# Moving the source-block one-hot rows behind a group's additions in the two edge layers of a graph network

## The reference, cut to what matters

```
def _rgcn_layer(x, W, SW, b, src, dst, rel):
    xt = jnp.einsum('nd,rde->rne', x, W)
    msg = xt[rel, src]
    agg = jax.ops.segment_sum(msg, dst, num_segments=x.shape[0])
    return jax.nn.relu(agg + x @ SW + b)
...
x = _rgcn_layer(x, w1, sl1, b1, src, dst, rel)
x = _rgcn_layer(x, w2, sl2, b2, src, dst, rel)
```

## Time and profile before

| | us |
|---|---|
| median of 3 runs | 9071.17 |
| lowest and highest | 9058.99, 9072.06 |
| span of the profiled execution | 9059.0 |
| time of the run that fits that execution | 9058.99 |
| gathers of layer one start, first to last | 120.3 to 2250.7 |
| gathers of layer two start, first to last | 2276.0 to 4383.8 |

### The profile page before, as it was taken

How to read it: one execution, slowest core, us unless ns; L and a number is a source line. 1 busy time by engine, 2 the same in 40 slices (tenths; PEclk the granted TensorE clock), 3 DMA queues, 4 the chain that set the end, 5 groups by cost and what they waited for, 6 DMA issues and landing times. The chain is left out here.

```text
span 9059.0 us, 172600 instructions
## 1 busy us (share of the span) xinstructions
PE 6437.7 (71%) x29604; PEld 5123.3 (57%) x29605; DVE 5894.2 (65%) x18020; ACT 2567.4 (28%) x6875; POOL 6592.5 (73%) x6759
## 2 busy tenths in 40 slices
PE   6555555555688888888788888888745666666657
PEld 4443333333455555555588888887635555555555
DVE  4444444444566666666688888888845666666667
ACT  3111111111011111111355555555433333333322
POOL 6777777777777777777677777777667777777752
PEclk7556666666555555555555555555556777777778
DMA  5222222222222222222355555555435665666653
GB/s 196 60 64 64 64 64 64 65 64 62 52 61 62 62 62 62 62 62 62 96 136 137 136 136 136 136 137 136 121 78 129 152 150 144 155 150 149 149 135 78
DMA packets 1031683, 926.16 MB, mean 102 GB/s; under 512 B 210913, under 2 KB 911477, under 8 KB 1031495
## 3 DMA queue, kind: packets, MB, share of 16 engines
q0 software_dynamic: 214496, 443.25, 17.7%
q1 hardware_dynamic: 627671, 341.67, 14.8%
q10 hardware_dynamic: 189400, 139.98, 7.5%
HBM read 734.34 MB, written 192.49 MB: 102 GB/s over the span
## 5 line engine op out<-in xcount | busy, mean ns | idle before, releaser
L597 PE MATMUL stage_ps_agg<-stage_hot,stage_msg 128*128 128x128 f32 x6656 | 1562.7, 409 | 1349.4 <-DMA stage_msg<-xt,stage_index 1004.4
L597 PEld LDWEIGHTS stage_ps_agg<-stage_hot,stage_msg 128*128 128x128 f32 x6656 | 1355.4, 302 | 1632.4 <-issue 624.3
L1613 POOL DMA_INDIRECT slots<-big,stage_index x1664 | 1656.3, 995 | 512.5 <-issue 449.9
L586 POOL DMA_INDIRECT stage_msg<-xt,stage_index x1664 | 1624.6, 976 | 530.0 <-issue 472.3
L1157 POOL DMA_INDIRECT big<-q,stage_index x1664 | 1594.4, 958 | 546.9 <-issue 490.2
L586 POOL DMA_INDIRECT stage_msg<-xt_next,stage_index x1664 | 1601.9, 963 | 531.1 <-issue 513.7
L621 DVE TENSOR_TENSOR big<-big,stage_ps_agg 128x128 f32 x3328 | 952.6, 286 | 1432.0 <-PE stage_ps_agg L597 1072.2
L575 ACT ACTIVATE stage_index<-big 128x4 int32 (+1 forms) x832 | 170.2, 205 | 3698.9 <-PE stage_ps_agg L597 3655.7
L1656 PE MATMUL stage_ps_val<-nodes_a,big 128*128 x3328 | 665.6, 362 | 506.1 <-ACT big L1576 481.7
L1656 PEld LDWEIGHTS stage_ps_val<-nodes_a,big 128*128 128x128 f32 x3328 | 566.2, 257 | 549.8 <-issue 544.5
L1666 PE MATMUL stage_ps_sums<-stage_hot,big 128*128 128x128 f32 x4160 | 737.1, 343 | 107.5 <-DVE big L1784 101.4
(11 more groups left out here) (302 smaller groups left out, 9639.0 us busy)
## 6 DMA issues: line engine op xcount, KB each, us to landing
big<-slots SPq DMA_DIRECT2D x1976, 66.0 KB
big<-in_edge_attr_dram SPq DMA_DIRECT2D x1664, 64.0 KB
stage_trow<-targets ACTq DMA_DIRECT2D x830, 128.0 KB
stage_msg<-xt,stage_index POOLq DMA_INDIRECT x1664
stage_msg<-xt_next,stage_index POOLq DMA_INDIRECT x1664
big<-q,stage_index POOLq DMA_INDIRECT x1664
slots<-big,stage_index POOLq DMA_INDIRECT x1664
xt_next<-stage_xo SPq DMA_DIRECT2D x98, 256.0 KB, 2.9
```

The lines of the kernel that those rows point to most:

```text
L586: pool.indirect_dma_start(self.msg[q][:, j, :], None, self.xt, bass.IndirectOffsetOnAxis(ap=self.index[q][:, j:j + 1], axis=0))\
L597: last = self.nc.tensor.matmul(self.ps[h][:, j, :], self.msg[q][:, j, :], self.hot[h][:, j, :], start=True, stop=True)
L1613: pool.indirect_dma_start(d["slots"], bass.IndirectOffsetOnAxis(ap=index[q][:, j:j + 1], axis=0), total[q][:, j, :], None).then_inc(s_sc[q ...
```

## The change

In both layers DVE makes `hot` of group x + 1 first as before, then adds group x, and only then makes `block_hot` of group x + 1. The waits that stood ahead of `block_hot` go with it, and in layer two `base` goes with it too. The added test of `x.edge(1)` is decided while the program is built. No instruction is added or taken away.

```diff
@@ first layer, DVE
             if x.edge(1):
                 v.wait_ge(a.s_freed, x.at(1) + SLOTS - 1)
                 a.make_hot(v, x)
-                if x.edge(-1):
-                    v.wait_ge(s_met, x.at(-1) + 1)
-                a.make_block_hot(v, x)
             if x.edge():
                 if x.near == 0:
                     v.wait_ge(s_clear, 1)
                 a.add_sums(v, x)
+            if x.edge(1):
+                if x.edge(-1):
+                    v.wait_ge(s_met, x.at(-1) + 1)
+                a.make_block_hot(v, x)
             if x.job(SUM):
@@ second layer, DVE
                 h = x.slot(1, 2)
                 v.wait_ge(a.s_freed, x.at(1) + SLOTS - 1)
                 a.make_hot(v, x)
-                if x.edge(-1):
-                    v.wait_ge(s_rank, x.at(-1) + 1)
-                    v.wait_ge(s_pick, x.at(-1) + 1)
-                a.make_block_hot(v, x)
-                nc.vector.tensor_scalar(base[h][:, :], t["ident"][0:W, 0:W], begin[:, bass.ds(x.at(1), 1)], None,
-                                        ALU.mult).then_inc(s_base, 1)
             if x.edge():
                 a.add_sums(v, x)
                 h = x.slot(0, 2)
@@
                 nc.vector.tensor_reduce(t["slot_of"][:, bass.ds(x.at() * G, G)], pick[:, :, :], AX.X, ALU.add)\
                     .then_inc(s_kept, 1)
+            if x.edge(1):
+                h = x.slot(1, 2)
+                if x.edge(-1):
+                    v.wait_ge(s_rank, x.at(-1) + 1)
+                    v.wait_ge(s_pick, x.at(-1) + 1)
+                a.make_block_hot(v, x)
+                nc.vector.tensor_scalar(base[h][:, :], t["ident"][0:W, 0:W], begin[:, bass.ds(x.at(1), 1)], None,
+                                        ALU.mult).then_inc(s_base, 1)
             if x.job(SUM):
```

## The result

The changed kernel takes 9093.31 us in the median of 16 runs (9083.87 to 9100.16), the kernel before 9074.22 us in 16 (9058.99 to 9084.69). The ratio is 1.002, 95% interval 1.0013 to 1.0028. So it is some 19 us **slower**, where I had forecast 11 us faster. The time lies inside the 9020 to 9098 us to which the rivals had widened the range, and outside the 9033 to 9086 us of the main case. The profiled execution has a span of 9089.4 us, 30 us more than that of before.

What follows compares the result with a forecast made beforehand. POOL's gather rhythm was taken to bound both layers, with only stretched gathers able to change: -6.6 and -4.5 us, -11 us in sum, from the runs' median 9071.17 to 9060 us; range 9033 to 9086, widened by rivals to 9020 to 9098.

Steps and rivals of the forecast that it cites:

- the main case: Both layers: shifted L603 lessens gather stretching by 11 us in sum, giving 9060 us; chance 0.50.
- What bounds the layers: Both layers: POOL never waits for a buffer, goes at 1.244 us a gather; only 78.6 us of stretching can change.
- The price of a place: One L603 starting a us ahead of a gather costs (0.57 - a) us, a from 0.04 to 0.57, nothing elsewhere.
- L610 alone: Rival: L610, now apart from L603, stretches gathers by itself; at most +1 us in sum, 9072 us; chance 0.03.
- Layer one: Layer one's stretching with L603 0.27 us later or less: 42 us in place of 48.7, so -6.6 us.
- Layer two: Layer two's stretching with L603 0.43 us later or more: 27 us in place of 31.0, so -4.5 us.
- the place of the earlier trace: Layer two, L603 0.44 us ahead of a gather: moves 0.54 us to behind its start, costs nothing instead of 0.13.
- they wait for PE anyway in most groups: DVE's additions of the next group come behind fewer instructions but still wait for PE, so nothing is gained there.
- My pass over the groups: All 832 groups worked through with additions where the trace has them, L603 shifted, stretches pushing later gathers: 42 and 27 us.
- The ends of 22 to 36 us: Layer two's range of stretching when the shifts are moved by 0.1 us either way.
- The rival "L603 lands just ahead of the starts": Smaller shift puts half of layer one's short-sum groups near the dear end: +32 us, 9103 us; chance 0.20.
- PE's wait for the base: Rival, layer two: the 0.9 us of cover is gone and PE waits for `base`: +83 us, 9154 us; chance 0.03.

Runs made afterwards that it cites:

- numbers_psum_c: Kernel before, with layer one's L603 reading its row of numbers from PSUM in place of SBUF; 11657.0 us against 11664.61, ratio 0.9996.
- two_ahead: Change in layer two alone, but `block_hot` and `base` made for group x + 2 with four buffers each; 11481.51 us against the kernel before's 11469.58, ratio 1.0011.
- ahead_of_pick: Change in layer two alone, but `block_hot` and `base` made between additions and pick; 11712.27 us against the kernel before's 11664.61, ratio 1.0039.
- before_again: The kernel before, unedited, run for its trace on one of the four other chips; 11668.23 us.

## Why the prediction was wrong

**What bounds the layers: right.** POOL's rhythm of 1.244 us and its stretching carried all of the two layers' difference on the chip of the forecast, to 0.1 us (24.0 us of busy time, 23.9 us of length in layer two).

**The price of a place: right.** 0.57 us less the distance fits the rows of after in both layers. It misses the few gathers of layer two that are held although L603 starts just behind them, or through two such instructions (4.6 us). numbers_psum_c and the trace of before show that the cause is L603's two SBUF inputs.

**L610 alone: small, as said.** After the change it stands apart from L603. The gathers that start while it runs, and over 0.12 us ahead of its end, are 32 in layer one with 2.1 us of stretching together and 44 in layer two with 2.3 us. Before the change they held 3.4 and 3.5 us.

**Layer one: too large.** -6.6 us was said, -2.4 us was measured, from one trace each. On the other chips POOL's busy time in layer one goes from 1608.9 to 1622.4 us with one and the same order, so the sign is not shown either.

**Layer two: the step that failed.** I said 31 to 27 us and it was 31.1 to 55.1. Two things in the working fell.

The first is the place of the earlier trace rows, a group with a job's sum: "It will start 0.01 to 0.10 us behind that gather's start and cost nothing in place of 0.13". That took a shift of 0.54 us ("that load runs 0.73 us from the instruction ahead of it and begins behind L610"). In the rows of after the shift is 0.33 us, so most of the load's time passes beside L610 and the base. L603 stays 0.22 us *ahead* of the gather in the median, in the dear part, and the place went from 11.6 to 29.1 us. I put the same 0.54 us on the places where the loop turns, and 0.44 us was measured.

The second is the start of the additions, "they wait for PE anyway in most groups". In layer one 410 of 416 groups do. In layer two 151 of 416 do, before the change. In three of the four places of the turn PE's sums have been there for 0.6 to 1.4 us (medians) when the additions start, so it is DVE's own chain of instructions that sets the start. My pass over the groups let these additions come 0.2 to 0.6 us later along with L603. The prediction did not say so; its text has them where the trace had them. In truth they came 0.1 us earlier, because only L603 stands ahead of them now and no longer L610 and the base.

The second decided the sign. Redone over the trace of before with the additions where the text has them, the pass gives 29 us for the old order, 61 us with the shifts of the prediction (0.43 and 0.54 us), 53 us with the measured ones (0.43, 0.33, 0.43 and 0.44 us), and 44 us with those and additions 0.1 us earlier. With the shifts of the prediction and additions 0.4 us later in three of the four places it falls to 18 us. These values are good to some 10 us. So the method held the right sign for layer two, and the 27 us did not follow from what the prediction describes. The ends of 22 to 36 us varied L603's shift alone and left out the additions, which is why they did not hold 55 us.

**The rival "L603 lands just ahead of the starts" is the one that came**, but in layer two and not in layer one. I had argued that layer two's rows are "already past the edge" from one row, with the 0.54 us. I gave this rival 0.20.

**PE's wait for the base: right for the chip of the forecast, wrong as a general answer.** There POOL's idle time did not move (531.1 and 531.2 us in layer two), and PE shows no wait for L610 or the base. "About 0.9 us of cover is left" was enough. On the four chips where engines fall behind each other by several us it was not, and on the one where two_ahead ran it is most of the loss in layer two, 27 of 39 us. I gave it 0.03. What makes the last 12 us of two_ahead is open, and so is why ahead_of_pick did not help.

**What stays unshown.** That places alone made the 19 us on the chip of the forecast is read from the two traces, gather by gather, and from the agreement of the pass with them. No experiment could be timed on such a chip.

## What to carry to other kernels

Where the indirect DMAs that GpSimd issues set the pace, a VectorE instruction with two SBUF inputs costs by *where* it starts: look for indirect DMAs longer than their median, and at which VectorE instruction runs when they start. Try taking away the second SBUF input before reordering, since the price of an order hangs on tenths of a us in where it lands (here the stretching fell, and no gain in time could be shown). Before carrying a start over from the old trace, see whether it waits for another engine there or follows from the engine's own chain. And a producer should not be moved to just ahead of its reader because the steady rhythm leaves 1 us of cover. Give it a buffer more, or leave it.

## What the runs showed of the hardware

A gather that starts while a VectorE instruction with two SBUF inputs runs gets 0.12 us far and is then held to that instruction's end, up to 0.53 us for one of 0.69 us. One that has started is not held, and the VectorE instruction keeps its 0.69 us. The exceptions are the few of layer two in which L603 starts up to 0.08 us behind the gather, directly behind another instruction, or in which two such instructions follow each other (0.91 us is the longest before the change). With one of the two operands in PSUM 37.5 of 43.6 us of this went away.

The same kernel took 9074 us on one chip and 11461 to 11665 us on four others, with the same median gather (944 to 947 ns) but with some 480 us of buffer waits in each layer in the trace of before_again and idle stretches of 1.0 to 2.7 us ahead of VectorE additions for which the profile shows no wait.
